# A mixer and a quantised FFN on one core: activations turned in f32, the layer norm of tiles 4 to 7 on VectorE, small numbers made by pairs

## The reference, cut to what matters

```
u  = silu(causal_conv4(ctx @ in_proj.T) + conv_b)          # 256 channels
dt = softplus(dt_low @ dt_proj.T + dt_b);  dt_low, B, C = rows of x_proj @ u
state[n] = exp(dt * A[n]) * state[n] + dt * u * B[n];  y = sum_n state[n] * C[n]
x += (y + D * u) * silu(layernorm(x))

def bitlinear(x, w, b):          # x: RMS norm, then rounded to 127 levels by row; w: -1, 0 or 1
    return quant(x * rsqrt(mean(x*x) + eps)) @ ternary(w).T + b
h = gelu(silu(bitlinear(layernorm(x), w1, b1)))            # 1024 wide
h = layer_norm(h) * ln_g + ln_b
x += bitlinear(h, w2, b2)
```

## Time and profile before

| | |
|---|---|
| median of 3 runs | 210.56 us (209.32 to 212.87) |
| profiled execution, its own time | 211.12 us |
| span, first to last instruction | 209.3 us |
| mean granted PE clock | 0.878 |
| PE busy | 162.5 us, 78% of the span |
| PEld busy | 118.5 us, 57% |
| DVE busy | 173.8 us, 83% |
| ACT busy | 162.5 us, 78% |
| POOL busy | 148.5 us, 71% |

### The profile page before, as it was taken

How to read it: one execution, slowest core, us unless ns; L and a number is a source line. 1 busy time by engine, 2 the same in 40 slices (tenths; PEclk the granted TensorE clock), 3 DMA queues, 4 the chain that set the end, 5 groups by cost and what they waited for, 6 DMA issues and landing times. The chain is left out here.

```text
span 209.3 us, 3383 instructions
## 1 busy us (share of the span) xinstructions
PE 162.5 (78%) x1158; PEld 118.5 (57%) x1158; DVE 173.8 (83%) x267; ACT 162.5 (78%) x262; POOL 148.5 (71%) x142
## 2 busy tenths in 40 slices
...
PEclk9999988999999995999985699999999956955559
...
GB/s 176 277 57 354 403 324 0 2 3 190 160 57 0 0 3 124 176 106 2 0 2 0 139 165 99 5 0 0 0 3 0 25 0 2 0 25 27 30 25 75
DMA packets 7137, 15.89 MB, mean 76 GB/s; under 512 B 904, under 2 KB 4432, under 8 KB 6992
## 3 DMA queue, kind: packets, MB, share of 16 engines
...
...
HBM read 14.56 MB, written 1.11 MB: 75 GB/s over the span
## 5 line engine op out<-in xcount | busy, mean ns | idle before, releaser
L793 POOL TENSOR_TENSOR st<-st,bc 128x1024 f32<-128x1024 f32 x32 | 76.1, 2393 | 19.9 <-DVE st L949 19.6
L949 DVE TENSOR_TENSOR_SCAN st<-dA,ps 128x1024 f32<-128x1024 f32 x32 | 71.9, 2273 | 2.1 <-PE ps L481 2.1
L481 PE MATMUL ps<-diagB,dtuT 64*128 64x128 f32 x512 | 47.0, 311 | 7.7 <-DVE st L949 6.3
L645 ACT ACTIVATE dA<-dt,negA 128x255 f32<-128x255 f32 x128 | 52.4, 494 | 0.1
L481 PEld LDWEIGHTS ps<-diagB,dtuT 64*128 64x128 f32 x512 | 35.6, 200 | 20.4 <-issue 8.7
L518 PE MATMUL ps<-id_f,st 128*128 128x128 f32 x256 | 35.8, 287 | 1.6 <-POOL st L793 1.6
L518 PEld LDWEIGHTS ps<-id_f,st 128*128 128x128 f32 x256 | 30.1, 148 | 4.3 <-POOL st L793 2.0
L558 PE MATMUL ps<-rows_sb,diag 128*128 128x512 f32 x32 | 17.4, 672 | 3.0 <-ACT w_raw L678 3.0
L576 PE MATMUL ps<-w2q,q2T 128*128 128x256 bf16 x64 | 11.8, 347 | 5.8 <-DVE res L1073 3.0
L1023 DVE BATCH_NORM_STATS2 stats<-w_raw 128x6 f32<-128x512 f32 x16 | 10.2, 678 | 5.0 <-ACT w_raw L682 5.0
L829 POOL TENSOR_TENSOR w_raw<-w_raw,rows_sb 128x1024 f32<-128x1024 f32 x6 | 14.1, 2354 | 0.0
...
## 6 DMA issues: line engine op xcount, KB each, us to landing
...
```

What stands on the lines that cost most here:

```text
L481: mm = nc.tensor.matmul(o[:, i:i + SG // 2, t, r, :], dtuT[rows, b % 2, h, t, :], diagB[rows, b % 2, t, n, :], start=True, stop=True)
L645: e = nc.scalar.activation(dA[:, k % DA_RING, i * L + 1:(i + 1) * L], dt[:, h, b % 2, 1:L], ACT.Exp, scale=negA[:, h, n:n + 1])
L793: tt(s, s, bc[:, ng].rearrange("p s l -> p (s l)"), ALU.mult).then_inc(prod_done, 1)
L949: nc.vector.tensor_tensor_scan(st[:, k % ST_RING, :], dA[:, k % DA_RING, :], slot(k), 0.0, ALU.mult, ALU.add).then_inc(scanned, 1)
```

## The change

It does the following:

- `q1` and `q2` are gone. `turn_q1` and `turn_q2` turn the f32 values, which still carry the rounding constant, and `copy_q1` and `copy_q2` subtract it on their way out of PSUM. `quant2` and the cast in `quant1` are gone.
- `LAST` is 4 instead of 6: DVE applies the layer norm of tiles 4 to 7.
- `root2a`, `root2b`, `out_scale` and `scales2` handle both tiles of a batch at once in batches 0 to 2, and one tile each for tiles 6 and 7.
- `clip_weights` moves from DVE to POOL.
- `diag` has 64 columns and the bias product is made in two 64 x 64 quarters.
- `gate` writes into `yT` in PSUM, `x1` reads it there, and `sum_states` of the next batch waits for `x1` instead of `gate`.
- All four tables are written anew.

```diff
 VECTOR_AT (entries 3, 8, 10, 11, 12, 15 to 32)
-3 "dt_mask:1 wmean:0 dt_sum:1"
-10 "dt_neg:2 clip_weights:0 gate:0 gate:1 x1:0"
-17 "quant1:0 clip_weights:1 spread_b:12 dt_mask:3"
-30 "scales2:1 bn2:3 gain:2"
-32 "bn2:4 bn2:5 gain:3 amax2:2 gate:6 gate:7 res:0 x1:6 x1:7 ln1:3 scales2:2 quant1:3 amax2:3 ... "
+12 "spread_b:10 x1:0 spread_b:11 x1:1 wmean:0 dt_sum:2"
+28 "bn2:3 ln1:2 quant1:2"
+29 "gain:2"
+31 "gain:3 amax2:2 res:0 bn2:4"
+32 "bn2:5 amax2:3 gate:6 gate:7 x1:6 scales2:1 x1:7 ln1:3 res:1 quant1:3 gain:4 gain:5 amax2:4 amax2:5 scales2:2
+    bn2:6 res:2 gain:6 bn2:7 res:3 gain:7 amax2:6 scales2:3 amax2:7 res:4 scales2:4 res:5 res:6 res:7"
 SCALAR_AT
+16 "silu_u:3 scale_weights:0"
+20 "dt_bias:3 scale_weights:1"
+24 "silu_z:2 silu:0 gelu:0 silu:1 gelu:1 copy_du:3"
+30 "norm:0 copy_q1:1 norm:1 silu_z:3 silu:2 gelu:2 square:0 square:1 silu:3 gelu:3 copy_z:3 scale2:0"
+32 "copy_q2:0 scale2:1 norm:2 copy_q2:1 norm:3 copy_q1:2 silu:4 square:2 gelu:4 silu:5 square:3 gelu:5
+    scale2:2 scale2:3 copy_q2:2 copy_q2:3 copy_q1:3 square:4 silu:6 square:5 gelu:6 silu:7 gelu:7
+    scale2:4 scale2:5 square:6 copy_q2:4 square:7 copy_q2:5 scale2:6 scale2:7 copy_q2:6 copy_q2:7"
 POOL_AT
+12 "clip_weights:0"
+16 "clip_weights:1"
+23 "root2a:0"
+24 "shift:0 shift:1"
+28 "root1:2 root2a:1 add_b2:0 out_scale:0"
+32 "root2b:1 add_b2:1 root2a:2 root1:3 out_scale:1 root2b:2 root2a:3 root2a:4 out_scale:2 root2b:3
+    add_b2:2 root2b:4 out_scale:3 add_b2:3 out_scale:4"
 PE_AT
+16 "b_cols:3 scale_rest:18 scale_b:19 scale_rest:19 mm1:0 scale_b:20"
+22 "scale_b:25 scale_rest:24 scale_rest:25 turn_q1:1 mm1:2 scale_b:26"
+28 "scale_rest:29 turn_q2:1 turn_q1:2 scale_b:30 scale_rest:30 mm1:4 mm2:0 scale_b:31 mm1:5 scale_rest:31"
+32 "mm2:1 turn_q2:2 turn_q2:3 turn_q1:3 mm1:6 mm2:2 mm1:7 mm2:3 turn_q2:4 turn_q2:5 mm2:4 turn_q2:6
+    mm2:5 turn_q2:7 mm2:6 mm2:7"
...
-        diag = sb("diag", [P, 2, P])
+        diag = sb("diag", [P, 2, HP])
-        LAST = TILES - TPB
+        LAST = 4
+        def span_of(g):
+            return (g, 0, TPB) if g < NB - 1 else (NB - 1, g - NB + 1, g - NB + 2)
...
-                        pe.wait_ge(gate_step, TPB * b)
+                        pe.wait_ge(x1_half, TPB * b)
...
-                        mm = nc.tensor.transpose(tq1[:, o:o + P], q1[:, t, h * P:(h + 1) * P], id_b[:, :])
+                        mm = nc.tensor.transpose(head[:, o:o + P], xc[:, t, h * P:(h + 1) * P], id_f[:, :])
...
-                    nc.tensor.matmul(big[:, c], diag[:, i, :], rows_sb[:, c], start=True, stop=False)
+                    for r in range(2):
+                        at = slice(r * HP, (r + 1) * HP)
+                        nc.tensor.matmul(big[at, c], diag[at, i, :], rows_sb[at, c], start=True, stop=False)
...
-                    mm = nc.tensor.transpose(tq2[:, k * P:(k + 1) * P], q2[:, t % 2, k * P:(k + 1) * P], id_b[:, :])
+                    mm = nc.tensor.transpose(big[:, k * P:(k + 1) * P], hid[:, t % HSLOTS, k * P:(k + 1) * P], id_f[:, :])
...
-                nc.scalar.activation(q2T[:, t % 2].rearrange("p k n -> p (k n)"), tq2, ACT.Copy).then_inc(q2T_done, 1)
+                nc.scalar.activation(q2T[:, t % 2].rearrange("p k n -> p (k n)"), big, ACT.Identity, bias=-ROUND).then_inc(q2T_done, 1)
...
-            def root2a(t):
+            def root2a(g):
+                _, lo, hi = span_of(g)
+                s = [sm2[:, lo:hi, j] for j in range(3)]
+                pool.wait_ge(mv2_done, upto(g))
+                ...
+                tt(s[1], s[0], m_half[:, lo:hi], ALU.pow).then_inc(root2a_step, 1 if on_act else 2)
...
-            def quant2(t):
-                ts(q2[:, t % 2, :], hid[:, t % HSLOTS], 1.0, -ROUND, ALU.mult, ALU.add).then_inc(q2_done, 1)
...
-                tt(yg[:, t, :], yT[:, t, :], siluzT[:, b, t, :], ALU.mult).then_inc(gate_step, 1)
+                tt(yT[:, t, :], yT[:, t, :], siluzT[:, b, t, :], ALU.mult).then_inc(gate_step, 1)
...
-                tt(x_nat[:, t, b, :], x_nat[:, t, b, :], yg[:, t, :], ALU.add).then_inc(x1_half, 1)
+                tt(x_nat[:, t, b, :], x_nat[:, t, b, :], yT[:, t, :], ALU.add).then_inc(x1_half, 1)
...
-                ts(q1[:, :, :], xc[:, :, :], ROUND, None, ALU.subtract).then_inc(q1_done, 1)
-                    ts(diag[:, i, :], id_f[:, :], s[7][:, i:i + 1], None, ALU.mult).then_inc(diag_done, 1)
+                    ts(diag[:, i, :], id_two[:, :], s[7][:, i:i + 1], None, ALU.mult).then_inc(diag_done, 1)
```

More of the change, by code:

```diff
@@ L68 @@
     "",
[19 rows of a table removed]
+    "dt_neg:2",
+    "spread_b:8",
+    "dt_mask:2",
+    "spread_b:9 gate:0 gate:1",
+    "spread_b:10 x1:0 spread_b:11 x1:1 wmean:0 dt_sum:2",
+    "",
+    "",
+    "ln1:0",
+    "",
+    "quant1:0 dt_neg:3",
+    "gate:2 x1:2 spread_b:12 gate:3",
+    "spread_b:13 x1:3 spread_b:14",
+    "dt_mask:3 spread_b:15",
+    "dt_sum:3 ln1:1",
+    "bn2:0",
+    "",
+    "bn2:1 quant1:1",
+    "gain:0 gain:1",
+    "gate:4 gate:5 amax2:0 bn2:2 x1:4 x1:5",
+    "amax2:1 scales2:0",
+    "bn2:3 ln1:2 quant1:2",
+    "gain:2",
+    "",
+    "gain:3 amax2:2 res:0 bn2:4",
+    "bn2:5 amax2:3 gate:6 gate:7 x1:6 scales2:1 x1:7 ln1:3 res:1 quant1:3 gain:4 gain:5 amax2:4 amax2:5 "
+    "scales2:2 bn2:6 res:2 gain:6 bn2:7 res:3 gain:7 amax2:6 scales2:3 amax2:7 res:4 scales2:4 res:5 "
+    "res:6 res:7",
 )
@@ L139 @@
     "",
-    "root1:0 add_b2:0",
+    "clip_weights:0",
+    "",
+    "root1:0",
+    "",
+    "clip_weights:1",
+    "",
+    "dt_series:3",
+    "root1:1",
     "",
@@ L143 @@
     "",
-    "dt_series:3",
-    "",
-    "",
[L147 to L152, removed]
-    "",
-    "root2b:1 root1:2 quant2:0",
-    "out_scale:1 root2a:2",
+    "root2a:0",
+    "shift:0 shift:1",
+    "root2b:0",
+    "",
+    "",
+    "root1:2 root2a:1 add_b2:0 out_scale:0",
+    "shift:2",
+    "shift:3",
+    "",
+    "root2b:1 add_b2:1 root2a:2 root1:3 out_scale:1 root2b:2 root2a:3 root2a:4 out_scale:2 root2b:3 "
+    "add_b2:2 root2b:4 out_scale:3 add_b2:3 out_scale:4",
+)
@@ new lines @@
+PE_AT = (
+    "xdbl:1 scale_b:1 turn_half:1 scale_rest:1 dtraw:1 scale_b:2 scale_rest:2 b_cols:1 convolve:2 "
+    "scale_b:3 scale_rest:3 scale_b:4",
+    "",
+    "scale_rest:4 turn_z:0 scale_b:5",
+    "scale_rest:5",
+    "xdbl:2 scale_b:6 turn_du:1 scale_rest:6 scale_b:7 dtraw:2 scale_rest:7 scale_b:8",
+    "scale_rest:8",
+    "b_cols:2 scale_b:9 scale_rest:9 scale_b:10",
+    "scale_rest:10 scale_b:11",
+    "scale_rest:11 scale_b:12 convolve:3 scale_b:13 wsum:0 scale_rest:12",
+    "scale_rest:13 turn_du:2",
+    "scale_b:14",
+    "scale_rest:14",
+    "turn_z:1 scale_b:15 scale_b:16 xdbl:3 scale_rest:15",
+    "scale_rest:16",
+    "dtraw:3 scale_b:17 scale_b:18 scale_rest:17",
+    "turn_q1:0",
+    "b_cols:3 scale_rest:18 scale_b:19 scale_rest:19 mm1:0 scale_b:20",
+    "scale_rest:20 mm1:1 scale_b:21",
+    "scale_rest:21 turn_du:3 scale_b:22",
+    "turn_z:2 scale_rest:22 scale_b:23",
+    "scale_rest:23",
+    "scale_b:24",
+    "scale_b:25 scale_rest:24 scale_rest:25 turn_q1:1 mm1:2 scale_b:26",
+    "",
+    "scale_rest:26 mm1:3 turn_z:3 scale_b:27",
+    "scale_rest:27 scale_b:28",
+    "scale_rest:28",
+    "scale_b:29 turn_q2:0",
+    "scale_rest:29 turn_q2:1 turn_q1:2 scale_b:30 scale_rest:30 mm1:4 mm2:0 scale_b:31 mm1:5 "
+    "scale_rest:31",
@@ L156 @@
     "",
     "",
-    "root2a:3 quant2:1 shift:2",
     "",
[L160 to L197, removed]
@@ L198 @@
+    "mm2:1 turn_q2:2 turn_q2:3 turn_q1:3 mm1:6 mm2:2 mm1:7 mm2:3 turn_q2:4 turn_q2:5 mm2:4 turn_q2:6 "
     "mm2:5 turn_q2:7 mm2:6 mm2:7",
@@ L226, in mixer_ffn @@
         id_f = sb("id_f", [P, P])
-        id_b = sb("id_b", [P, P], BF16)
         ones = sb("ones", [P, P])
@@ L667, in copy_q1 @@
                     act.wait_ge(mm1_done, TPB * b)
-                nc.scalar.activation(q1T[:, :, :, :].rearrange("p t h n -> p (t h n)"), tq1[:, 0:TPB * HALVES * P],
-                                     ACT.Copy).then_inc(q1T_done, 1)
+                nc.scalar.activation(q1T[:, :, :, :].rearrange("p t h n -> p (t h n)"), head, ACT.Identity,
+                                     bias=-ROUND).then_inc(q1T_done, 1)
             def silu(t):
@@ L854, in quant2, with root2b @@
-            def quant2(t):
-                pool.wait_ge(w_done, t + 1)
-                if t >= 2:
-                    pool.wait_ge(q2_turned, t - 1)
-                ts(q2[:, t % 2, :], hid[:, t % HSLOTS], 1.0, -ROUND, ALU.mult, ALU.add).then_inc(q2_done, 1)
-            work = {"dt_series": dt_series, "root1": root1, "add_b2": add_b2, "root2a": root2a, "shift": shift,
-                    "root2b": root2b, "out_scale": out_scale, "quant2": quant2}
+            def root2b(g):
+                _, lo, hi = span_of(g)
+                s = [sm2[:, lo:hi, j] for j in range(7)]
+                pool.wait_ge(sq_done, upto(g))
+                if g:
+                    pool.wait_ge(sc2_step, 2 * first_use(g))
+                    pool.wait_ge(out_scaled, 2 * first_use(g))
```

(25 more changed lines are left out.)

147 lines of the change are left out of this document (59 added, 88 removed), and 73 rows, old and new, of tables (SCALAR_AT, VECTOR_AT).

## The result

The changed kernel took 217.06 us, the median of 4 runs (214.59 to 222.1), and the kernel before, timed beside it, 210.09. The ratio is 1.0305, 95% interval 1.0184 to 1.0427: slower, though whether by more than 2% the interval leaves open, where 205.3 us was forecast and 199.0 to 212.5 given as the range. In a second series the same kernel, unedited, took 218.48 (214.3 to 222.64) against 211.16, ratio 1.0206 (1.0085 to 1.0327). Executions fall into a faster and a slower state: medians here are of all, ratios of the faster ones alone, without the changed kernel's 222.1, 220.13 and 222.64.

A forecast was written before the change was run, and what follows sets the result against it. DVE bounds the scan stage, a chain of handovers the tail. Last scan 154.3, rounding 165.0, last gelu 184.9, plus 17.0: end 201.9, span 204.0, with 1.8 around it 205.8, less 0.56 for the median: 205.3 us; range 199.0 to 212.5.

The forecast's parts named there:

- The clip's price: Clip on POOL: four instructions of 2048 columns at 2.1 us, 8.3 in all, taken as covered and priced at 0.
- Rival "same": In-order waits for the second clip, at POOL's entry 16, take the scan stage's gain: 4.2 us, 209.5 us; chance 0.27.
- No wait of DVE over 3 us: Sign for the scan stage: new waits of 1 us or less at four places, 2 to 3 us at the last.
- last scan ends: End of the scan stage: 157.1 less 2.8 us, at 154.3 us.
- DVE busy, 25.5 us to there: DVE's busy time up to the last scan: from 122.4 us down by 2.7, some 119.7.
- batch 3 rounded: Tail after the last scan: DVE's 8.6 us of work from 156.4, rounded at 165.0, before at 170.6.
- last gelu ends: Tail from batch 3's rounding through turns, copies, bias product and activations: 184.9 us, against 188.3 before.
- from there to the last `res`: Kernel's end after the last gelu: 17.0 us, against 18.9 before.
- The bias products: PE, eight 64-row instructions for four of 128, halves overlapping in part: 2.85 us at the higher clock, +0.9.
- slower rival: Bias products' quarters on PE don't overlap at all: 3.96 us each at the higher clock, 212.8 us in all; chance 0.15.
- `x1` from PSUM: DVE's six `x1` in the scan stage fall from 0.589 to at most 0.48 us, 0.7 us together.
- faster rival: Longer PE work holds the clock at the higher level from `mm1:6`: 199.0 us; chance 0.15.

The follow-up runs named there:

- Experiment three: Changed kernel with both instructions of each clip on POOL as multiply-add, weights rounded but not clipped to -1..1; 203.25 us, ratio 0.9707.
- experiment seven: Changed kernel with the clip on POOL as multiply-add (weights not clipped) and nine memsets of 1024 columns between its two instructions; 216.9 us, ratio 1.0276.
- experiment eight: Kernel before with six subtract-max instructions of 512 columns on POOL in the idle start, six small DVE instructions beside them; no whole time given.

## Why the prediction was wrong

**The clip's price, the step that failed.** "nearest is 1.04 us for 1024 columns, so 2.1 each, 8.3 in all ... I price it at 0". The row was a multiply-add; the clip is subtract-max and min. Measured: 7.1 and 5.4 us each, 24.9 in all. The row nearest in shape was not nearest in arithmetic, and there was no second row of POOL to bound it from above. The bound that was given, "without cover both clips, 8.3 us, would show", was a bound on the cover and not on the price. Experiment three has the forecast's price and gives 203.25 us; experiment seven has POOL busy as long as it really was, by other instructions, and gives 216.9. The one term carries the 12 us between forecast and result. Against the clip's time on POOL the ratio to the kernel before is 0.9707 at 7.6 us, 1.0305 and 1.0206 at 24.9 and 1.0543 at 29.8: up to 24.9 that is 0.6 to 0.7 us for each us more, and beyond it steeper.

**The mechanism.** Rival "same" had the place, `mm1:0` behind `clip_weights:1` and the scan's input behind it, with 4.2 us; it was 6.8 in the changed kernel and 15.2 in experiment two. The text saw that products stand behind the clip too, and argued from slack ("may lag scans by three units"), which held for 3.8 us of work at a time (experiment three) and not for 12.5. "No wait of DVE over 3 us" fell. The text also said that the engines get in each other's way and that the clip is four more instructions that can do so, and put nothing into the sum for it. The rule that it took from the Trainium skill (SBUF — State Buffer, "Who interferes with whom") it gave without its condition: there a DVE instruction with one SBUF input is exempt only outside the 2-port modes, and `tensor_scalar` is named among those that can enter them. This case agrees with the page and not with the short form: `xc` (L992), a TENSOR_SCALAR with one tensor from SBUF, took 4.99 us beside the clip where 0.35 is usual. Not everything agrees: by the page the product of two SBUF tensors in experiment eight contends too, and it took its usual 0.41 us.

**The rest of the sum,** read in experiment three, which has the clip at the forecast price:

| step | forecast | experiment three |
|---|---|---|
| last scan ends | 154.3 | 154.40 |
| DVE busy, 25.5 us to there | 119.7 | 124.00 |
| batch 3 rounded | 165.0 | 164.44 |
| last gelu ends | 184.9 | 180.54 |
| from there to the last `res` | 17.0 | 16.7 |
| span | 204.0 | 199.4 |

The first row is right by two misses that cancel (the text's own 2.7 us, not 2.8, would give 154.4). DVE was busy 4.3 us more: 1.9 of it is `gain` of tile 2, beside a POOL product that ends at 141.87 (3.21 us where 1.3 is usual, first row below); the rest was not taken apart. Its waits were 4.9 us in all, not 9. The `gain` of tiles 4 and 5, for which the forecast said that they would wait for POOL, were not held: each instruction took 1.28 us (second row), with POOL idle beside them. The last gelu came 4.4 us early, half of it by one bias product, which took 3.09 us where the text has 5.3 at the lower clock (second fence, the same kernel's PE).

```profile
139.74 3.21 DVE L1045 TENSOR_TENSOR w_raw<-w_raw,rows_sb 128x1024 f32<-128x1024 f32 x1 [0.36 <-ACT w_raw L694]
...
164.88 1.28 DVE L1037 SCALAR_TENSOR_TENSOR w_raw<-w_raw,mv,rows_sb 128x1024 f32<-128x1024 f32 x1
```
```profile
167.13 3.09 PE L564 MATMUL ps<-rows_sb,diag 64*64 64x512 f32 x8 [0.35 <-ACT q2T L718]
```

**The bias products.** Forecast 2.85 us at the higher clock, by the slower rival 3.96. The PE timeline of the changed kernel (216.82 us) has, at the higher clock and for comparison the f32 turns:

```profile
113.60 1.93 PE L564 MATMUL ps<-rows_sb,diag 64*64 64x512 f32 x8
...
205.37 1.94 PE L575 MATMUL ps<-id_f,w_raw 128*128 128x128 f32 x8 [1.16 <-ACT w_raw L711]
208.76 1.04 PE L575 MATMUL ps<-id_f,w_raw 128*128 128x128 f32 x8
```

Eight quarters take 1.93 us, no more than the four whole ones before (1.98): the two halves overlap fully though they write one bank. (Each of the eight takes 0.59 us by itself, as each of the four did, so they can't have run one after the other in 1.93.) The slower rival falls, and the rule that the prediction weighed (the Trainium skill, TensorEngine Tiling (Array Packing), "Gotcha 1: PSUM Pressure") is not borne out by this row, in which the halves write different partitions of the bank. The f32 turns, 1.04 and 1.94, were forecast at 1.0 and 2.0.

**`x1` from PSUM** took 0.41 us each, not over 0.48, and no two took 1.9: right. **Clock:** the faster rival's clock came in part. From batch 3's rounding to the last gelu it was 0.80 in the changed kernel and 0.82 in experiment three, where the kernel before had 0.69; behind the last gelu 0.68 and 0.66 against 0.62. In the changed kernel the lower clock also came behind PE's waits for the clip: the bias product after 6.46 us of waiting took 3.62 instead of 1.93.
